# Conv and mixture-of-experts kernel: all up matmuls of a tile, then all its down matmuls, with the last block of the inner width filled up to 128 rows

## The reference

```python
def _L0_ffn_ref(x, router_w, w1, w2, w3):        # 8 experts, C = 64, inner width 682
    ...
    h1 = jnp.einsum('nc,ehc->neh', flat, w1)
    h3 = jnp.einsum('nc,ehc->neh', flat, w3)
    h = jax.nn.silu(h1) * h3
    y = jnp.einsum('neh,ech->nec', h, w2)
    out = jnp.einsum('ne,nec->nc', gates, y)
```

## Time and profile before

| | us |
|---|---|
| median of 3 runs | 1052.32 |
| lowest, highest | 1051.89, 1053.75 |
| span of the profiled execution | 1053.6 |
| PE busy | 932.6 (89%) |
| DVE busy | 627.8 (60%) |
| POOL busy | 611.6 (58%) |
| ACT busy | 500.6 (48%) |

### The profile page before, as it was taken

The page is one execution under the profiler, slowest core; times in us unless marked ns, Lnnn a source line. Parts: engine busy times, 40 slices in busy tenths (PEclk is TensorE's granted clock), DMA queues, the critical chain, the costliest instruction groups (busy, mean ns, idle before and its releaser), DMA issues.

```text
span 1053.6 us, 18732 instructions
## 1 busy us (share of the span) xinstructions
PE 932.6 (89%) x4463; PEld 542.0 (51%) x4463; DVE 627.8 (60%) x1475; ACT 500.6 (48%) x858; POOL 611.6 (58%) x649
## 2 busy tenths in 40 slices
PE   4968798882899999999999999999999999999723
PEld 2753266651455555555454545454545467777512
DVE  3775589798555555555555555555555555555457
ACT  3214444332456565656565656565656565555300
POOL 3640017777777777777777777776653333434452
PEclk9888899795799999999999999999999999999955
DMA  7100023342343444443434343434343356565177
GB/s 171 23 1 1 0 73 127 130 135 90 125 132 118 133 118 132 118 133 117 134 117 134 117 131 119 131 119 128 111 126 105 120 166 195 170 197 182 50 246 233
DMA packets 72237, 129.24 MB, mean 123 GB/s; under 512 B 15861, under 2 KB 47790, under 8 KB 72208
## 3 DMA queue, kind: packets, MB, share of 16 engines
q1 hardware_dynamic: 50448, 107.10, 33.4%
q0 software_dynamic: 17408, 17.62, 5.0%
q10 hardware_dynamic: 4352, 4.20, 1.5%
HBM read 99.67 MB, written 29.71 MB: 123 GB/s over the span
## 4 chain that ended last, share of the span: by engine, by line
PE 77%; DVE 11%; issue 5%; DMA 2%; ACT 1%; SPq 1%; POOL 1%; DVEq 1%; ACTq 0%; POOLq 0%
PE bank L1405 35%; PE bank L1420 26%; PE bank L1384 4%; PE bank L1307 3%; PE bank L1432 3%; PE bank L1321 1%; PE bank L1258 1%; PE bank L1326 1%; DMA y_and_rows<-expert_w 1%; DVE stats L1003 1%; PE bank L1242 1%; DMA y_and_rows<-result_rows 1%; DVE y_and_rows L1203 1%; PE bank L1247 1%; ACT quant_tmp L666 1%
## 5 line engine op out<-in xcount | busy, mean ns | idle before, releaser
L1157 DVE TENSOR_TENSOR conv_all<-conv_all,bank 128x512 f32<-128x512 f32 (+1 forms) x408 | 280.6, 688 | 319.2 <-PE bank L1405 165.4
L583 POOL DMA_INDIRECT result_rows<-conv_all,dest_now x272 | 272.1, 1000 | 199.4 <-DVE conv_all L1165 122.5
L726 ACT ACTIVATE conv_all<-bank 128x512 f32<-128x512 f32 (+1 forms) x408 | 243.6, 597 | 186.8 <-PE bank L1405 184.3
L1405 PE MATMUL bank<-xT_hi_lo,w 128*128 128x512 f32 (+1 forms) x748 | 307.1, 411 | 2.4 <-issue 1.9
L563 POOL DMA_INDIRECT expert_rows<-rows_now,slot_now x256 | 248.1, 969 | 86.5 <-issue 68.9
L1405 PE MATMUL bank<-xT_lo_hi,w 128*128 128x512 f32 (+1 forms) x748 | 280.7, 375 | 0.0
L1420 PE MATMUL bank<-conv_all,w 128*64 128x512 f32 (+3 forms) x816 | 267.1, 579 | 0.5 <-DVE conv_all L1157 0.5
L1405 PEld LDWEIGHTS bank<-xT_hi_lo,w 128*128 128x128 f32 x748 | 141.6, 189 | 120.8 <-DVE conv_all L1157 90.6
L1405 PEld LDWEIGHTS bank<-xT_lo_hi,w 128*128 128x128 f32 x748 | 141.9, 190 | 17.3
L1420 PEld LDWEIGHTS bank<-conv_all,w 128*64 128x64 f32 (+1 forms) x816 | 52.7, 134 | 116.6 <-issue 111.8
L740 ACT ACTIVATE conv_all<-bank 128x512 f32<-128x512 f32 x68 | 40.6, 597 | 132.1 <-PE bank L1420 132.1
(11 more groups left out here) (247 smaller groups left out, 975.0 us busy)
## 6 DMA issues: line engine op xcount, KB each, us to landing
w<-expert_w SPq DMA_DIRECT2D x68, 704.0 KB, 4.2
w<-expert_w SPq DMA_DIRECT2D x68, 192.0 KB, 2.4
y_and_rows<-result_rows SPq DMA_DIRECT2D x16, 512.0 KB, 6.5
conv_all<-expert_rows SPq DMA_DIRECT2D x56, 132.0 KB
expert_w<-w_stacked SPq DMA_DIRECT2D x8, 704.0 KB
result_rows<-conv_all,dest_now POOLq DMA_INDIRECT x272
w_split<-expert_w SPq DMA_DIRECT2D x6, 704.0 KB, 4.2
w_stacked<-expert_w SPq DMA_DIRECT2D x6, 704.0 KB, 4.1
```

The lines of the kernel that those rows point to most:

```text
L583: nc.gpsimd.indirect_dma_start(yout, bass.IndirectOffsetOnAxis(ap=destc[u][:, g:g + 1], axis=0), yrow[u][:, g, :], None, bounds_check=2 * ...
L726: nc.scalar.activation(sbuf[k % 3][0:m, :], h1_ps[k % 3][0:m, :], ACT.Silu).then_inc(silu_rdy, 1)
L1157: V.tensor_tensor(hbuf[(2 * u + k) % 4][0:m, :], sbuf[k % 3][0:m, :], h3, ALU.mult).then_inc(mul_rdy, 1)
L1405: ins = mm(ps[k % 3][:, rows_], wbuf[i][u][:, 128 * c:128 * c + 128], xT[p][u][:, rows_], start=p == 0, stop=p == 1)
```

## The change

The inner activations of a tile get six buffers, one for each block, and the order becomes all six ups, then `turn` of the next tile, then all three downs, on every engine. The sixth buffer lies on `wide`, which the first stage has done with; a memset zeroes it once, so that rows 42 to 127 stay zero, and the last `down` reads all 128 rows of it and of `w2` (whose rows beyond 42 are zero in both versions). `turn` and `rows_out` trade places on the bank they share, so their waits move by one tile.

```diff
-        hbuf = [carve(T) for u in range(4)]
+        hbuf = [carve(T) for k in range(HT)] + [wide[:].rearrange("p g c -> p (g c)")[:, 0:T]]
...
             def tile(j, u, two, first=False, last=0):
                 if not first:
                     copy_y(j - 1, 1 - u)
-                if last != 1:
-                    copy_xT(j + 1, 1 - u, 0)
-                silu(j, 2)
-                if last != 1:
-                    copy_xT(j + 1, 1 - u, 1)
-                for k in range(3, KT):
+                for k in range(KT):
                     silu(j, k)
                 if last != 1:
-                    silu(j + 1, 0)
-                    silu(j + 1, 1)
...
+                    copy_xT(j + 1, 1 - u)
...
             pipelined(dve, spread, norm, NP)
+            V.memset(hbuf[HT], 0.0)
...
-                dve.wait_ge(w2_rdy, KT // 2 * j + k // 2 + 1)
-                V.tensor_tensor(hbuf[(2 * u + k) % 4][0:m, :], sbuf[k % 3][0:m, :], h3, ALU.mult).then_inc(mul_rdy, 1)
+                dve.wait_ge(w2_rdy, KT // 2 * j + k // 2)
+                V.tensor_tensor(hbuf[k][0:m, :], sbuf[k % 3][0:m, :], h3, ALU.mult).then_inc(mul_rdy, 1)
...
             def tile(j, u, two, first=False, last=0):
+
+                for k in range(KT):
+                    hidden(j, u, k)
+                    if k == 1 and not first:
+                        rows_out(j - 1, 1 - u)
                 if not last:
                     split(j + 2, u, two[2])
-                for k in range(2, KT):
-                    hidden(j, u, k)
-                    if k == 4 and not first:
-                        rows_out(j - 1, 1 - u)
-                if last != 1:
-                    hidden(j + 1, 1 - u, 0)
-                    hidden(j + 1, 1 - u, 1)
...
                 pe.wait_ge(split_rdy, j + 3)
                 if not first:
-                    pe.wait_ge(yr_sb, j)
+                    pe.wait_ge(yr_sb, j + 1)
...
                     for i in range(k, k + 2):
-                        m = 128 if i < HT else HR
                         h = 64 * (i % 2)
-                        ins = mm(y_ps[h:h + 64, rows_], w2buf[e][u][0:m, i, :], hbuf[(2 * u + i) % 4][0:m, rows_],
+                        ins = mm(y_ps[h:h + 64, rows_], w2buf[e][u][:, i, :], hbuf[i][:, rows_],
                                  start=i < 2 and e == 0, stop=i >= KT - 2 and e == two)
...
                 if not last:
-                    pe.wait_ge(xt_sb, j + 3)
+                    pe.wait_ge(xt_sb, j + 2)
...
             def tile(j, u, two, first=False, last=0):
+                for k in range(KT):
+                    up(j, u, k, two[0])
+                    if k == 2 and not first:
+                        rows_out(j - 1, 1 - u)
                 if last != 1:
                     turn(j + 1, 1 - u, first)
-                up(j, u, 2, two[0])
-                up(j, u, 3, two[0])
-                down(j, u, 0, two[0])
-                up(j, u, 4, two[0])
-                if not first:
-                    rows_out(j - 1, 1 - u, last == 1)
-                up(j, u, 5, two[0])
-                down(j, u, 2, two[0])
-                if last != 1:
-                    up(j + 1, 1 - u, 0, two[1])
-                    up(j + 1, 1 - u, 1, two[1])
-                down(j, u, 4, two[0])
+                for k in range(0, KT, 2):
+                    down(j, u, k, two[0])
```

More of the change, by code:

```diff
@@ L726, in silu, with copy_xT @@
                 nc.scalar.activation(sbuf[k % 3][0:m, :], h1_ps[k % 3][0:m, :], ACT.Silu).then_inc(silu_rdy, 1)
[L728 to L735, removed]
+            def copy_xT(j, u):
+                act.wait_ge(xt_rdy, j + 1)
+                nc.scalar.activation(xT[0][u][:], turn_ps[:], ACT.Copy)
+                nc.scalar.activation(xT[1][u][0:C, :], turn_ps[C:2 * C, :], ACT.Copy)
+                nc.scalar.activation(xT[1][u][C:2 * C, :], turn_ps[0:C, :], ACT.Copy).then_inc(xt_sb, 1)
             def copy_y(j, u):
@@ L744, in tile @@
                     copy_y(j - 1, 1 - u)
-                if last != 1:
-                    copy_xT(j + 1, 1 - u, 0)
-                silu(j, 2)
-                if last != 1:
-                    copy_xT(j + 1, 1 - u, 1)
-                for k in range(3, KT):
+                for k in range(KT):
                     silu(j, k)
                 if last != 1:
-                    silu(j + 1, 0)
-                    silu(j + 1, 1)
[L756 to L759, removed]
+                    copy_xT(j + 1, 1 - u)
+            copy_xT(0, 0)
             tiles(act, tile)
@@ L1168, in tile @@
             def tile(j, u, two, first=False, last=0):
+                for k in range(KT):
+                    hidden(j, u, k)
+                    if k == 1 and not first:
+                        rows_out(j - 1, 1 - u)
                 if not last:
                     split(j + 2, u, two[2])
-                for k in range(2, KT):
-                    hidden(j, u, k)
-                    if k == 4 and not first:
-                        rows_out(j - 1, 1 - u)
-                if last != 1:
-                    hidden(j + 1, 1 - u, 0)
-                    hidden(j + 1, 1 - u, 1)
             split(0, 0)
             split(1, 1)
-            hidden(0, 0, 0)
-            hidden(0, 0, 1)
             tiles(dve, tile)
@@ L1436, in tile @@
             def tile(j, u, two, first=False, last=0):
+                for k in range(KT):
+                    up(j, u, k, two[0])
+                    if k == 2 and not first:
+                        rows_out(j - 1, 1 - u)
                 if last != 1:
                     turn(j + 1, 1 - u, first)
-                up(j, u, 2, two[0])
-                up(j, u, 3, two[0])
-                down(j, u, 0, two[0])
-                up(j, u, 4, two[0])
-                if not first:
-                    rows_out(j - 1, 1 - u, last == 1)
-                up(j, u, 5, two[0])
-                down(j, u, 2, two[0])
-                if last != 1:
-                    up(j + 1, 1 - u, 0, two[1])
-                    up(j + 1, 1 - u, 1, two[1])
-                down(j, u, 4, two[0])
+                for k in range(0, KT, 2):
+                    down(j, u, k, two[0])
             turn(0, 0, True)
-            up(0, 0, 0)
-            up(0, 0, 1)
             tiles(pe, tile)
```

## The result

| | before, us | after, us |
|---|---|---|
| median (lowest, highest) of 4 runs | 1053.03 (1051.89, 1054.07) | 1004.40 (1003.69, 1006.75) |
| span of the profiled execution | 1053.6 | 1002.4 |
| PE, DVE, POOL, ACT busy | 932.6, 627.8, 611.6, 500.6 | 834.3, 622.3, 610.3, 492.7 |
| DVE's reduce in `rows_out` of tiles 0, 49, 67 | 289.25, 806.55, 996.07 | 281.31, 783.98, 943.92 |

A forecast was written before the change was run, and what follows sets the result against it. PE, 89% busy, was taken as the bound, with POOL as slow through tile 39. 20.3 us at tile 51, 6.9 in five full and 20.0 in twelve half tiles, less 0.5, took 46.7 from 1052.3: 1006 us, range 997 to 1022.

The forecast's parts named there:

- Pairing: Last down group: with 128 rows its two matmuls run together, saving 1.00 us a full tile, 1.29 a half-expert tile.
- no pairing: Rival, last down group: the pair stays apart for a reason other than K, giving 1034 us; chance 0.07.
- The order: PE's tile: two groups of up matmuls instead of four, fewer switches, saving 0.38 us a tile.
- POOL's hold: Scatters: POOL at 10.64 us a tile holds PE through `rows_out`'s wait for tile j-2; 20.3 us won at tile 51.
- The stall before `up(j, 5)`: Rival: DVE's order costs PE 0.5 to 0.9 us a tile there, giving 1015 to 1022 us; chance 0.10.
- The half tiles' loads: Rival: loads keep half-expert tiles at their old pace, so 20.0 us go, giving 1026 us; chance 0.07.
- The clock: Rival: PE idles about 1.5 us a tile behind POOL, the clock drops, slower than before; chance 0.03.
- The sum: Whole kernel: 20.3 us at tile 51, 6.9 in full tiles, 20.0 in half tiles, less 0.5: 46.7 us saved.

The follow-up runs named there:

- new_order_42: The kernel after with the last down reading 42 rows of block 5 again, order and buffers new: 1277.2 us, ratio 0.9744 to the kernel before in its group.
- before_ring4: The kernel before with four buffers for result rows and their addresses in place of two: 1303.7 us, ratio 0.9981 to the kernel before.

## Why the prediction was right, step by step

**Pairing: right.** The last down group fell by 1.00 us in a full tile (new_order_42 against the kernel after: 0.99). "Only K differs" was the ground for taking it; the experiments narrow it to 42 or 64 rows beside 128, which the prediction had left unsaid. The Trainium skill's "TensorEngine Tiling (Array Packing)", section "Theoretical Speedup", which gives small contract dimensions up to twice the speed, had spoken for the rival "no pairing" (42 rows as the form to keep); here the 42-row group takes 2.01 us and the 128-row group 1.01.

**The order: right in sign, the term mis-sized.** I had 0.38 us a tile, from two up groups instead of four. It is 0.57 (10.54 to 9.97 in new_order_42). The ups are right: in the timeline of the kernel after they take (810.00 - 807.10) + (812.82 - 810.35) = 5.37 us, for 5.39. What failed are the two other terms of the tile, which the sum carried over unchanged. The downs had 1.01 us each, from a down between ups, 3.03 for three; three in a row take 2.72, that is 0.91 each. And `turn`, now ahead of downs and not of ups, takes 804.38 - 803.85 = 0.53 us, where it had 0.41 before (505.34 to the first up at 505.75). 9.17 - 0.31 + 0.12 - 0.02 = 8.96, and 8.97 was measured. In half-expert tiles the difference shows as 9.05 us on the mean ((937.35 - 846.87) / 10, the reduces of tiles 56 and 66) against 10.94 before: 1.89 saved instead of 1.67, over 12 tiles 2.7 us.

**POOL's hold: right, and nearly exact.** Predicted and measured, in us:

| | predicted | measured |
|---|---|---|
| start of tile 39's last scatter | 707.2 | 707.43 |
| a tile of the padding loop | 9.26 | 9.24 |
| start of tile 47's last scatter | 781.3 | 781.39 |
| DVE's reduce of tile 49 | 783.4 | 783.98 |
| won at the start of tile 51 | 20.3 | 20.2 (before: 811.38 - 2.05 = 809.33; after: 789.14) |

Part of this exactness is luck. The stripe copy at 284.95 started at 283.15 before, so POOL's work begins 1.8 us later, and its turn of four tiles is 0.17 us shorter than I took (42.39 for 42.56), which gives 1.7 back over ten turns. DVE's reduce comes 2.6 us after tile 47's last scatter starts and not 2.1, and from there to tile 51 there are 789.14 - 783.98 = 5.16 us and not 5.6 (whose own terms, 1.5, 0.5, 0.5 and 3.0, add up to 5.5); so 20.2 is 22.6 - 2.4 where I had 23.1 - 2.8. The wait in `rows_out` began at tile 3 and not "near the tenth": reduces stand 8.90, 8.91, 9.42, 9.96 and 10.27 us apart from tile 0 on, and the 47 waits are one for each tile from 3 to 49. POOL was already behind when the loop began: it starts tile 0's scatters at 291.75, 10.4 us after the reduce that they need (281.31). I had not looked at where POOL would stand when PE starts. It cost nothing in the sum, which was made from POOL backwards.

**The stall before `up(j, 5)`: right.** Where POOL doesn't hold PE the profile shows none: from 790 to 835 us PE is busy for 45.00 of 45.00 and has no wait.

**The half tiles' loads: right.** PE is busy for 108 of 110 us at 200 GB/s in the last stretch above.

**The clock: the rival's mechanism was there, its price not.** The prediction had counted a granted clock below 1.00 in the loop as a sign of being wrong. It came, six times (0.65 and 0.78 in the stretches above), and cost nothing that can be seen. After the wait that ends at 341.67, with the lower clock, DVE's next reduces stand 10.89, 9.60, 10.28 and 11.58 us apart, together 42.35; after the one that ends at 426.29, without it, 10.27, 10.26, 10.27 and 11.59, together 42.39. What the slow matmuls lost came out of the time that PE would have stood waiting for POOL.

**The sum.** From the last scatters on:

- at tile 51, 20.2 us (predicted 20.3);
- from there to the last reduce: before 996.07 - 809.33 = 186.74, after 943.92 - 789.14 = 154.78, so 32.0 (predicted 26.9; 0.9 more in five full tiles, 2.7 in twelve half tiles; the remaining 1.5 isn't traced to one place);
- behind the last reduce 58.5 us instead of 57.5: 1.0 lost, not foreseen, in the gather and the output;
- the memset took 0.49 us on DVE for the 0.5 of the sum, but POOL's times from tile 39 on don't show it.

The first three make 20.2 + 32.0 - 1.0 = 51.2 us between the two spans, 4.5 more than the 46.7 of the sum. Between the medians it is 48.6 (47.9 against the 1052.3 from which I subtracted). The step that failed on this side is taking the median as 1.3 us less than the span: that distance was one between different executions, and the text ahead of the prediction has the span as the profiled execution's own time, which the record doesn't have. The kernel after's profiled execution has a span of 1002.4 and a time of 1004.2, 1.8 more and close to its median; if that holds for the kernel before too, which no run shows, its profiled execution took 1055.4, longer than all four of the result. So two errors, 4.5 us too little saved and 3.3 us too much taken as its share of the median (51.2 against 47.9), leave the forecast within 2 us of the result.

## What to carry to other kernels

When an engine is "58% busy", look at what it is doing between two of its waits: here issuing 128-row indirect scatters took POOL 1.3 us each, 0.98 of it busy, and it was full. If a second engine is nearly as slow as the first, make the sum backwards from the second one's fixed work, not as tiles times what the first one saves. And look in a timeline for two matmuls that should overlap and don't: filling one with zero rows so that both have as many was worth more here (0.97 us a tile) than the whole new order (0.57).

## What the runs showed of the hardware

- Two matmuls with 64 output columns each, which write different halves of a bank's 128 rows, overlap if both have 128 rows of contraction (1.01 us for the four records between ups, 0.91 in a row) or both have 64 (2.87 for the three downs, against 2.72). 42 beside 128 and 64 beside 128 don't: 3.71 for the three downs in both. Here fewer rows are slower than more.
- A down group in a row with others costs 0.10 us less than one between up matmuls (0.91, 1.01); the `turn` ahead of them costs 0.12 more than one ahead of ups (0.53, 0.41).
- PE stood for 0.4 to 2.4 us in 32 tiles up to 47, and the granted clock was 0.98 (600 to 700). Up to tile 47 it fell only behind waits of 2.4 us, and behind six of the nine: to 0.76 over 7 us. A turn of four tiles took as long with it as without (42.35 and 42.39).
- The kernel before took 1284 to 1307 us in the groups of the experiments and 1053 for the result, with the difference ahead of tile 0 and in tiles 0 to 40 (before_ring4 beside before). What binds in the one (POOL) doesn't bind in the others. Whether that is the chip or something else, and what stalls the tiles, stays open.
